# Second layer of a macaron block: twelve tiles in its second routed set and four dense tiles, in place of ten and six

## What is computed

```python
def _L0_ffn_ref(x, gate_w, w1, w2, w3):
    flat = x.reshape(-1, d)
    probs = jax.nn.softmax(flat @ gate_w.T, axis=-1)
    weights, idx = jax.lax.top_k(probs, TOPK)          # 2 of 8
    weights = weights / jnp.sum(weights, axis=-1, keepdims=True)
    combine = jnp.sum(jax.nn.one_hot(idx, E, dtype=flat.dtype) * weights[..., None], axis=1)
    h1 = jnp.einsum('nd,ehd->neh', flat, w1)           # hidden size 256
    h3 = jnp.einsum('nd,ehd->neh', flat, w3)
    y = jnp.einsum('neh,edh->ned', jax.nn.silu(h1) * h3, w2)
    return jnp.einsum('ned,ne->nd', y, combine)

x = x + 0.5 * _L0_ffn_ref(_layernorm(x), gate_w, w1, w2, w3)
x = x + _L0_attn_ref(_layernorm(x), WQ, WK, WV, WO)
x = x + 0.5 * _L0_ffn_ref(_layernorm(x), gate_w, w1, w2, w3)
```

## Time and profile before

| | us |
|---|---|
| three runs | 619.85, 624.39, 625.75 |
| their median | 624.39 |
| the profiled execution's own time | 619.24 |
| its span, from first to last instruction | 617.5 |
| PE busy | 517.3 (84%) |
| DVE, ACT, POOL busy | 374.3, 310.2, 267.6 |
| second layer's units, first to last down projection | 463.3 to 610.8 |

### The profile page before, as it was taken

The page is one execution under the profiler, slowest core; times in us unless marked ns, Lnnn a source line. Parts: engine busy times, 40 slices in busy tenths (PEclk is TensorE's granted clock), DMA queues, the critical chain, the costliest instruction groups (busy, mean ns, idle before and its releaser), DMA issues.

```text
span 617.5 us, 19023 instructions
## 1 busy us (share of the span) xinstructions
PE 517.3 (84%) x7286; PEld 416.7 (67%) x7286; DVE 374.3 (61%) x995; ACT 310.2 (50%) x597; POOL 267.6 (43%) x325
## 2 busy tenths in 40 slices
PE   1779879999998578888888886777689899999995
PEld 1667858779987345555556564545368789989994
DVE  5633933333355778888989988666346343355665
ACT  4853524344334156666666765556553244345543
POOL 6865764630654033434342110554614530556562
PEclk9999988999998679999999999999989999999999
DMA  9941223546865222656212020311033546653232
GB/s 275 329 150 39 53 68 91 137 108 145 154 151 144 72 60 72 170 155 189 90 50 85 16 88 2 115 36 37 31 74 93 144 124 122 152 131 99 66 90 56
DMA packets 114662, 65.87 MB, mean 107 GB/s; under 512 B 51856, under 2 KB 108432, under 8 KB 114576
## 3 DMA queue, kind: packets, MB, share of 16 engines
q1 hardware_dynamic: 107664, 50.49, 31.1%
q0 software_dynamic: 6912, 14.17, 8.6%
HBM read 18.88 MB, written 34.87 MB: 87 GB/s over the span
## 4 chain that ended last, share of the span: by engine, by line
PE 37%; DVE 16%; issue 4%; ACT 3%; another core or an unknown queue 1%; DMA 1%; POOL 0%; DVEq 0%; ACTq 0%; POOLq 0%
PE bank L1621 9%; DVE negmax L1302 7%; PE bank L1502 5%; PE bank L1504 5%; PE bank L1503 5%; PE bank L1734 2%; PE bank L1797 2%; ACT pt L950 2%; PE bank L1764 2%; PE bank L1812 1%; PE bank L1751 1%; PE bank L1800 1%; DVE rden L1319 1%; PE bank L1514 1%
## 5 line engine op out<-in xcount | busy, mean ns | idle before, releaser
L1189 DVE SCALAR_TENSOR_TENSOR pt<-bank,pt 128x512 f32<-128x512 f32 x122 | 84.3, 691 | 154.5 <-PE bank L1504 72.6
L694 POOL DMA_INDIRECT yg<-sorted_y,row x108 | 104.3, 965 | 145.8 <-PE bank L1621 65.7
L950 ACT ACTIVATE pt<-bank 128x768 f32<-128x768 f32 x128 | 103.8, 811 | 88.0 <-PE bank L1773 83.1
L680 POOL DMA_INDIRECT sorted_x<-xs,row x108 | 106.2, 983 | 78.9 <-DVE pt L1189 33.0
L1621 PE MATMUL bank<-w,pt 128*128 (+1 forms) x976 | 133.1, 279 | 8.5 <-issue 7.3
L1621 PEld LDWEIGHTS bank<-w,pt 128*128 128x128 f32 x976 | 120.5, 193 | 14.1 <-issue 10.0
L1302 DVE TENSOR_REDUCE negmax<-bank 128x10 f32<-128x640 f32 x128 | 104.2, 818 | 30.2 <-PE bank L1751 26.4
L833 ACT ACTIVATE pt<-bank 128x512 f32<-128x512 f32 x122 | 73.2, 600 | 50.0 <-PE bank L1504 37.3
L841 ACT ACTIVATE yb<-bank 128x256 f32<-128x256 f32 x82 | 31.5, 384 | 76.6 <-PE bank L1621 50.7
L1734 PE MATMUL bank<-zc 63*64 63x64 f16 (+3 forms) x1024 | 44.1, 250 | 30.4 <-DVE negmax L1302 24.8
L1734 PEld LDWEIGHTS bank<-zc 63*64 63x64 f16 x1024 | 19.3, 107 | 58.1 <-DVE negmax L1302 38.7
(11 more groups left out here) (171 smaller groups left out, 1022.6 us busy)
## 6 DMA issues: line engine op xcount, KB each, us to landing
sorted_y<-yb SPq DMA_DIRECT2D x82, 128.0 KB
zc<-qk_rows SPq DMA_DIRECT2D x96, 64.0 KB
sorted_x<-zeros SPq DMA_DIRECT2D x2, 2944.0 KB, 14.1
qk_rows<-qksplit SPq DMA_DIRECT2D x8, 512.0 KB
sorted_x<-zeros SPq DMA_DIRECT2D x1, 2432.0 KB, 11.5
sorted_x<-zeros SPq DMA_DIRECT2D x1, 2176.0 KB, 10.2
X<-x_in SPq DMA_DIRECT2D x8, 256.0 KB, 5.1
zc<-w_up SPq DMA_DIRECT2D x8, 256.0 KB, 6.1
```

Of the source, the lines that this page charges most:

```text
L680: ps.indirect_dma_start(out=sorted_x[s], out_offset=bass.IndirectOffsetOnAxis(ap=row[:, s, k, t:t + 1], axis=0), in_=xs[:, R0[s] + t, :], ...
L694: ps.indirect_dma_start(out=yg[:, a % D_YG, k, :], out_offset=None, in_=sorted_y[s], in_offset=bass.IndirectOffsetOnAxis(ap=row[:, s, k, t ...
L950: s_.activation(pt[:, hg, (u % 2) * 768:(u % 2 + 1) * 768].rearrange("p (a n) -> p a n", a=2), bank[:, B_ST:B_ST + 2, 0:384], ACT.Exp, sca ...
L1189: v_.scalar_tensor_tensor(hid[:, n % D_HID], bank[:, B_H3 + n % 2, :], 1.0 / WSCALE, silu[:, n % D_H], ALU.mult, ALU.mult).then_inc(prod_d ...
```

## The change

Set 3 takes two tiles more, 16 to 27 in place of 16 to 25: 19 units in place of 17. Tiles 28 to 31 stay dense: 2 blocks, 16 units in place of 24. Due times of the second layer's gathers become 7 d // 13 (56 gathers in place of 52), those of the 24 scatters 5 d // 10. The output's order is written anew.

```diff
-RT = (12, 16, 16, 10)
+RT = (12, 16, 16, 12)
 SETS, SECOND = 4, 2
-D0 = (12, 26)
-DT = (4, 6)
+D0 = (12, 28)
+DT = (4, 4)
...
         def gather_unit(p, d):
-            return U_TILE[3] + 2 + 9 * d // 13 if p else U_TILE[1] + 2 + 7 * d // 10
+            return U_TILE[3] + 2 + 7 * d // 13 if p else U_TILE[1] + 2 + 7 * d // 10
...
             for t in range(0, 12, TILES):
                 routed_finished(2, t, TILES)
-            dense_finished(0)
             routed_finished(2, 12, TILES)
             routed_finished(3, 0, TILES)
+            dense_finished(0)
+            routed_finished(3, 4, TILES)
+            routed_finished(3, 8, TILES)
             dense_finished(1)
-            routed_finished(3, 4, TILES)
-            routed_finished(3, 8, 2)
-            dense_finished(2)
-            sp.wait_ge(out_done, 16 * 10)
+            sp.wait_ge(out_done, 16 * 9)
...
             for d in range(2 * RT[3]):
-                pool.wait_ge(prod_done, done(U_TILE[2] + LAG + 6 * d // 10, D_H))
+                pool.wait_ge(prod_done, done(U_TILE[2] + LAG + 5 * d // 10, D_H))
                 scatter(3, d // 2, ks=[d % 2])
```

## The result

The change made the kernel slower: **635.56 us** (median of 4 runs, 634.79 to 638.6) against 624.52 (4 runs of the kernel before on the same chip), a ratio of 1.021 with a 95% interval of 1.016 to 1.025 (ratios are estimated from the single runs, so they differ a little from the quotient of the two medians, here 1.018). The forecast was 610.8 us and faster. The profiled execution took 636.04 us, with a span of 634.3.

The account below looks back on a forecast made before the run. PE's down projections every 2.20 us were taken as the bound. Last sum -11.75, output +0.3, selection +0.1 gave -11.3 us: 607.9 us profiled, plus offset 2.9, 610.8 us; range 605.0 to 617.5 us.

Parts of the forecast that it names:

- Units: Second layer's dense and routed units: six fewer at 2.204 us each take 13.2 us off PE's path.
- The second rival: Second layer's gathers run slower than back to back: 610.2 us with late landings, 613.5 us with wider intervals; chance 0.18.
- the four cases: Forecast (0.58), PE alone setting the end (0.17), gathers slower than back to back (0.18), four buffers closing a loop (0.05).
- first gather against the kernel before: Start of the second layer's gathers: unchanged at 527.50, since the units ahead stay; 0 us.
- first gather to last: Second layer's 56 gathers: from 527.50 to 598.3, 1.25 us apart with one wait at the ninth.
- last gather's start to the last sum's end: End of the routed chain: 2.45 us to the landing, then a sum of 0.73 us, ending at 601.5.
- last sum to the span's end: Output's tail: 4.2 us as before, plus 0.3 us for 128 KB more in the first of two transfers.
- one wait: With 4 buffers of gathered rows, the ninth gather waits for the first tile's sum and starts at 539.5.
- The estimate of 2.45 us: Last gather's start to its landing: 0.94 us of instruction plus 1.5 us, as SP waits for the last output.
- The estimate of 2.15 us: A gather's 64 KB by the skill page's fixed cost and rate; last sum would end at 601.2, 0.3 earlier.
- PE alone as the end: Gathers land sooner or POOL misses the ninth gather's wait, so PE sets the end: 606.4 us; chance 0.17.
- The loop of four buffers: Every pair of gathers waits for the sum four tiles back, 0.6 us more per pair: 622 us; chance 0.05.

Follow-up runs that it names:

- 620 kind: Chips where the kernel before takes 616 to 625 us; the changed kernel, run there unaltered, took 635.6 against 624.5 us and 632.6 against 619.1 us.
- the runs with the paces alone: Kernel before with only the new due times of gathers and scatters, no tiles moved: ratio 1.031 where it takes 616.3 us, 0.996 where it takes 571.2 us.
- 571 kind: Chips where the kernel before takes about 571 us; the changed kernel, run there unaltered, took 561.26 against 570.98 us, ratio 0.982.
- the kernel with memsets: Changed kernel with each of the second layer's 56 gathers replaced by an equally long POOL memset: 610.34 us, ratio 0.990 to the kernel before.

## Why the prediction was wrong

**The sign.** The step that failed is the term *Units*, "Six fewer: 6 x 2.204 = 13.2 us off PE's path", which takes it that PE keeps its 2.20 us per unit beside a POOL whose gathers go back to back. The coupling between the two was put at nothing without a reason. Measured, that term is +17.3 us in place of -13.2 on the 620 kind (the table below), and taking out the 56 gathers gives back 24.1 us. The second rival does think of late gathers, but only by way of DVE's sums ("so nothing is added to it"). None of the four cases had this mechanism.

**The trace had shown it.** In the kernel before, each of the four runs of five scatters in the second layer had a gap of PE behind it (1.04, 0.83, 1.14 and 0.76 us), while the gathers in threes had nearly none. The chain of waits and the stretch from 560 to 604 us at a full 44.00 were read where POOL paused, and I carried their 2.20 us over to a POOL that does not pause. The change moves runs of five to runs of six and of three to runs of four to eight. The idle time that POOL's old pace left, 1.2 us behind each two or three gathers, looked like slack; by the runs with the paces alone it was what kept PE going.

**Term by term.** The 571 kind shows the sum without the stalls. The changed kernel's end there:

```profile
553.49 0.94 POOL L693 DMA_INDIRECT yg<-sorted_y,row  x1 [0.30 <-issue]
...
555.98 0.74 DVE L1197 SCALAR_TENSOR_TENSOR X<-yg,weight,X 128x128 f32<-128x128 f32 x2 [1.26 <-DMA yg<-sorted_y,row]
556.75 0.92 SPq L561 DMA_DIRECT2D out<-X  x2
```

| term | predicted | 571 kind | 620 kind |
|---|---|---|---|
| units, from the layer's first down projection to PE's last | -13.2 | 139.7 to 126.4: -13.3 | 147.7 to 165.0: +17.3 |
| first gather against the kernel before | 0 | +0.8 (counted from the layer's first down) | +5.2 (+6.2 counted so) |
| first gather to last | 70.8 | 70.1 | 93.7 |
| last gather's start to the last sum's end | 3.2 | 3.2 | 3.4 |
| last sum to the span's end | 4.5 | 4.5 | 4.5 |

On the 571 kind every term fits within 1 us, and the end is the one forecast: gathers 1.25 us apart, the last landing in 2.46 us, the last sum 2.0 us behind the last dense one. Two details are not. The first gather was released by the landing of the set's stores, not by its due time, which is the 0.8. And the wait of the ninth gather for a sum, the "one wait" that is "certain", cost nothing: it started 0.30 us behind the eighth, 10.7 us behind the first and not 12.0. That the chain as a whole still comes within 0.7 us is in part luck: the second gather came 0.6 us late and the 47 intervals behind the ninth took 59.4 us, 0.6 more than forecast. The change gained 9.7 us there, against 11.3 predicted, mainly because the kernel before is quicker there too: 83.4 us from its first gather to its last sum, where the trace of the prediction had 85.75. On the 620 kind the span missed by 634.3 - 606.2 = 28.1 us: the first gather was 5.2 us late (532.70, not 527.50, behind PE's stalls beside the scatters), and the gathers' chain took 22.9 longer; the last two terms held.

**The landing.** The estimate of 2.45 us is confirmed: 2.45, 2.46, 2.47, 2.51, 2.54 and 2.61 us for the last gather in six chains. The estimate of 2.15 us, worked out from figures in the Trainium skill's page "DMA: Bandwidth & Descriptors" (anatomy of one DMA on the GpSimd path), is too short here; the rows decide.

**The rivals.** PE alone as the end (0.17): no; even on the 571 kind PE ends 2.6 us before the last gather starts. Slower gathers (0.18): single ones keep 1.25 us within a run; the waits between runs grow. The loop of four buffers (0.05) has a grain of truth: POOL waited for sums five times, 13.7 us in all. But on the 571 kind seven such waits make 2.1 us, each the 0.30 that stands between any two gathers, so the buffers don't close a loop by themselves; the sums were late because PE's products were.

**The range.** It lay between 605.0 and 617.5, since every case began with PE at 2.20 us. The list of what would be wrong named "PE idle before down projections", and that is what came. A small slip in the number itself: the gain of 11.3 us is 1.8%, but 610.8 us is 2.2% below the median of 624.39, since only part of the profiled execution's offset of 5.15 was added back.

What stays open: why an unbroken series of indirect transfers stops PE, mostly 5.4 to 8.3 us in, and why only on some chips. PE is not alone in it. In the gaps beside the first run of six scatters the others start nothing either, though the last product of the unit ahead had ended at 473.78; POOL goes on:

```profile
475.05 0.96 POOL L679 DMA_INDIRECT sorted_x<-xs,row  x1 [0.30 <-issue]
476.03 0.60 ACT L832 ACTIVATE pt<-bank 128x512 f32<-128x512 f32 x1 [4.65 <-remote]
477.50 1.20 SPq L467 DMA_TRANSPOSE qksplit<-sorted_x  x1
477.56 0.69 DVE L1188 SCALAR_TENSOR_TENSOR pt<-bank,pt 128x512 f32<-128x512 f32 x1 [4.84 <-remote]
```

Which of them are stopped themselves and which only wait for another, the rows don't tell. Two explanations find no support in the traces. The transfers' packets don't take longer: those of 4096 bytes took 237 ns on average in the changed kernel's first trace, and 252 on the 571 kind. And it is not the loading of instructions: the kernel with memsets has as many packets of that queue (61 of 16 KB) as the changed kernel and no gap beside its memsets, and on the 571 kind they take as long (1.15 us against 1.08).

## What to carry to other kernels

Idle time of an engine beside the bound may be what keeps the bounding engine at its pace: before tightening a pace, look in the trace for the few places where that engine already runs without a break, and read what the bounding engine does there. Idle time marked as released by nothing, in small pieces, can be a coupling that no sum of durations holds; give it a case of its own, with a price from such a place. And when a gain rests on the chip's undisturbed pace, the same change can move the time by -1.8% on one chip and by +2.1% on another, so compare it on several.

## What the runs showed of the hardware

- The same kernel takes 571 us on three chips and 616 to 625 on others, with the DMA packets as fast on both (4096 bytes: 252 and 237 ns); on the slower ones PE has 13 to 30 us of gaps over 0.25 us in its unit stages, on the others 0 to 1.5.
- There, indirect transfers of POOL in runs of five and more stop PE in all but 4 of 85 cases, the first gap mostly 5.4 to 8.3 us into the run (72 of 81), for 1.4 us (5 and 6) to 2.9 us (7 and more) on average; memsets of the same length don't, and a quarter of the bytes changes nothing.
- Behind such gaps the granted clock falls to 0.5: for 23.0 of the 165.0 us of the changed kernel's second layer, and for none of its 126.4 us on the 571 kind. An fp16 product of 128x256 then takes 0.42 us in place of 0.27.
